# Cross-attention scores from float32r parts of queries and keys, three products in place of one float32 product

## What is computed

```python
q = (layernorm(x) @ Wq.T + bq).reshape(B, L, 16, 16)       # L = 64 queries
k = (ctx @ Wk.T + bk).reshape(B, S, 16, 16)                # S = 256 keys
v = (ctx @ Wv.T + bv).reshape(B, S, 16, 16)
scores = einsum('blhe,bshe->bhls', q, k)
attn = softmax(scores * 16 ** -0.5, axis=-1)
x = x + einsum('bhls,bshe->blhe', attn, v).reshape(B, L, 256) @ Wo.T + bo
```

## Time and profile before

| what | us |
|---|---|
| median of 3 runs | 950.61 |
| lowest and highest of these | 948.52, 951.25 |
| the profiled execution, its time | 948.79 |
| the profiled execution, its span (first to last instruction) | 947.0 |

### The profile page before, as it was taken

One profiled execution on the slowest core, in us unless ns is written; L12 is line 12 of the kernel. 1 busy time (PEld: TensorE's weight loads), 2 busy tenths in 40 slices (PEclk: granted clock), 3 DMA queues, 4 the chain that ended last, 5 costly groups with the idle time before them and its releaser, 6 DMA issues. The chain is left out here.

```text
span 947.0 us, 29217 instructions
## 1 busy us (share of the span) xinstructions
PE 888.6 (94%) x9714; PEld 722.3 (76%) x9730; DVE 790.7 (83%) x1711; ACT 690.9 (73%) x1983; POOL 344.8 (36%) x487
## 2 busy tenths in 40 slices
PE   5899999999999999999999988999999987999997
PEld 4788888888888888888888876878787863555554
DVE  3788878888888888887788877988888876999997
ACT  3587776776777767777677665777777765988887
POOL 1322322223222232224322337767666632222221
PEclk9999999999999999999999999999999997999999
DMA  9111111111111111111111000000000000000001
GB/s 303 37 39 39 43 34 40 40 39 34 39 39 44 39 34 39 39 44 39 34 39 39 28 1 2 1 2 0 1 0 1 2 1 1 28 28 28 28 28 39
DMA packets 31618, 31.64 MB, mean 33 GB/s; under 512 B 3280, under 2 KB 30800, under 8 KB 31568
## 3 DMA queue, kind: packets, MB, share of 16 engines
q1 hardware_dynamic: 30720, 30.73, 10.5%
q10 hardware_dynamic: 848, 0.33, 0.1%
HBM read 26.86 MB, written 4.19 MB: 33 GB/s over the span
## 5 line engine op out<-in xcount | busy, mean ns | idle before, releaser
L485 ACT ACTIVATE probs<-psum,nmax 128x256 f32<-128x256 f32 x512 | 237.8, 488 | 89.6 <-DVE nmax L445 89.6
L445 DVE TENSOR_REDUCE nmax<-psum 128x2 f32<-128x512 f32 x256 | 159.0, 684 | 30.8 <-PE psum L315 30.8
L328 PE MATMUL psum<-id_sb,probs 128*128 128x128 f32 x1024 | 136.4, 277 | 14.3 <-ACT probs L485 14.1
L328 PEld LDWEIGHTS psum<-id_sb,probs 128*128 128x128 f32 x1024 | 111.8, 141 | 30.3 <-ACT probs L485 29.2
L493 POOL TENSOR_TENSOR rstd<-vare,minus_half 128x1 f32<-128x1 f32 x96 | 52.9, 551 | 182.2 <-DVE vare L382 179.7
L502 POOL TENSOR_TENSOR cl<-c_sb,ch 128x512 fp32r<-128x512 f32 x64 | 81.7, 1276 | 99.8 <-ACT ch L460 99.8
L485 ACT ACTIVATION_READ_ACCUMULATOR probs<-psum,nmax 128x1 f32 x512 | 112.7, 220 | 0.0
L466 ACT ACTIVATE probsT<-psum 128x512 f32<-128x512 f32 x160 | 91.0, 625 | 9.0 <-PE psum L328 8.9
L509 POOL TENSOR_TENSOR rm<-rinv,hm_sb 128x256 f32<-128x256 f32 x64 | 39.8, 622 | 127.7 <-DVE rinv L421 127.7
L315 PE MATMUL psum<-k_sb,qb 32*128 32x256 f32 x1024 | 78.4, 404 | 0.0
L1006 PE MATMUL psum<-wb_all,xqT 128*128 128x512 bf16 x240 | 66.2, 390 | 10.3 <-DVE probs L906 7.0
(11 more groups left out here) (126 smaller groups left out, 2303.5 us busy)
## 6 DMA issues: line engine op xcount, KB each, us to landing
c_sb<-in_ctx_t SPq DMA_DIRECT2D x64, 256.0 KB, 2.7
x_sb<-in_x SPq DMA_DIRECT2D x32, 128.0 KB, 2.0
out<-y_sb SPq DMA_DIRECT2D x32, 128.0 KB, 1.7
w_all<-in_w_gate SPq DMA_DIRECT2D x1, 1024.0 KB, 7.9
w_all<-in_w_up SPq DMA_DIRECT2D x1, 1024.0 KB, 10.0
w_all<-in_w_down SPq DMA_DIRECT2D x1, 1024.0 KB, 12.5
wqkv_sb<-in_w_qkv SPq DMA_DIRECT2D x1, 768.0 KB, 6.3
wq_sb<-in_wq ACTq DMA_DIRECT2D x1, 256.0 KB, 3.9
```

The costliest lines, as they stand in the source:

```text
L328: last = nc.tensor.transpose(sp[g][:, c:c + P], probs[:, 2 * g + u, kh * P:(kh + 1) * P], id_sb[:])
L445: nc.vector.tensor_reduce(nmax[:, 2 * g:2 * g + 2], sp[g].rearrange("p (u s) -> p u s", u=2), AX.X, ALU.max, negate=True).then_inc(max_don ...
L485: nc.scalar.activation(probs[:, j, :], sp[g][:, u * S:(u + 1) * S], ACT.Exp, bias=nmax[:, j:j + 1], accum_out=rsum[:, j:j + 1]).then_inc(e ...
```

## The change

Queries and keys are split into a high part in float32r and a low part that holds the rest, and the scores become three float32r products (high by high, high by low, low by high) that accumulate in PSUM. ACT writes the high part of the keys from PSUM with the bias (two instructions of 128x256 a sequence) and the high part of the queries (one of 128x512 a tile). DVE writes the low part of the keys from PSUM (two instructions of 128x256 a sequence in place of one of 128x512). POOL writes the low part of the queries (one of 128x512 a tile). The scores wait for the low parts. In the order of the engines, the new ACT steps stand ahead of the copies to probsT; on DVE, the keys of sequence 1 move from ahead of the reciprocals and the first copy to probsT to behind them. To make room in SBUF, kbd4 now lies in the first part of w_all, and POOL waits for the quantized weights before it writes there.

```diff
@@ names
-        qb = [sb(f"qb{m}", [P, 2, 2, L]) for m in range(KT)]
-        k_sb = sb("k_sb", [P, KT, S])
+        qb = sb("qb", [P, KT, 2, 2, L])
+        qh, ql = sb("qh", [P, KT, 2, 2, L], F32R), sb("ql", [P, KT, 2, 2, L], F32R)
+        kh_sb, kl_sb = sb("kh_sb", [P, KT, S], F32R), sb("kl_sb", [P, KT, S], F32R)
-        kbd4 = [sb(f"kbd4{s}", [P, KT, 4, P]) for s in range(2)]
+        kbd4 = [w_all[:, 2 * i:2 * i + 2, :].rearrange("p k (h t) -> p k h t", h=4) for i in range(2)]
@@ pe_scores
-            pe.wait_ge(qb_done, t * 4 + 4)
+            pe.wait_ge(ql_done, t + 1)
             pe.wait_ge(k_ev, b + 1)
             for m in range(KT):
+                for n, (q, k) in enumerate(((qh, kh_sb), (qh, kl_sb), (ql, kh_sb))):
+                    for c in range(4):
+                        if m + n == 0 and (not isinstance(b, int) or b > 0):
+                            moved, count = pt_count(t + s - 1, 1 - s, c)
+                            pe.wait_ge(moved, count)
+                        rows = slice(32 * c, 32 * c + 32)
+                        last = nc.tensor.matmul(sp[c][:, m * S:(m + 1) * S],
+                                                q[rows, m, s, :, :].rearrange("p h q -> p (h q)"),
+                                                k[rows, m, :], start=n == 0, stop=n == 2)
@@ new steps
+        def dve_kl(v, t, s):
+            v.wait_ge(kh_done, (t * 2 + s) * KT + KT)
+            for m in range(KT):
+                last = nc.vector.scalar_tensor_tensor(kl_sb[:, m, :], k_ps[:, m, :], bk_sb[:, m:m + 1],
+                                                      kh_sb[:, m, :].bitcast(F32), ALU.add,
+                                                      ALU.subtract)
+            last.then_inc(k_ev, 1)
+        flat = "p m s h q -> p (m s h q)"
+        def act_qh(a, t):
+            a.wait_ge(qb_done, t * 4 + 4)
+            a.wait_ge(s_mm, t * 8)
+            nc.scalar.activation(qh[:].rearrange(flat), qb[:].rearrange(flat),
+                                 ACT.Copy).then_inc(qh_done, 1)
+        def act_kh(a, t, s):
+            a.wait_ge(k_mm, t * 2 + s + 1)
+            a.wait_ge(s_mm, (t * 2 + s) * 4)
+            for m in range(KT):
+                nc.scalar.activation(kh_sb[:, m, :], k_ps[:, m, :], ACT.Identity,
+                                     bias=bk_sb[:, m:m + 1]).then_inc(kh_done, 1)
+        def pool_ql(p, t):
+            p.wait_ge(qh_done, t + 1)
+            nc.gpsimd.tensor_tensor(ql[:].rearrange(flat), qb[:].rearrange(flat),
+                                    qh[:].rearrange(flat).bitcast(F32),
+                                    ALU.subtract).then_inc(ql_done, 1)
@@ vector body(t)
-                    dve_k(v, t, 1)
                     dve_inverse(v, t, 0)
                     dve_pt(v, t, 0, (0,))
+                    dve_kl(v, t, 1)
                     dve_xn(v, LN1, t + 1, x_sb[:], xt_mm)
@@ vector body(t), later
-                    dve_k(v, t + 1, 0)
+                    dve_kl(v, t + 1, 0)
                     dve_v(v, t + 1, 0)
@@ scalar body(t)
+                    act_kh(a, t, 1)
                     act_pt(a, t, 0)
...
                     act_exp(a, t, 1, (t, 0))
+                    act_qh(a, t + 1)
+                    act_kh(a, t + 1, 0)
                     act_pt(a, t, 1)
@@ gpsimd body(t)
                     pool_c(p, t + 1, 0)
+                    pool_ql(p, t + 1)
                     pool_rm(p, t, 1)
@@ gpsimd, start of the second stage
+                p.wait_ge(wq_step, 36)
                 pool_kbd4(p, 0, 0, 0, 0)
```

More of the change, by code:

```diff
@@ L212, in block_kernel @@
         cl_done = sem("cl_done")
+        qh_done = sem("qh_done")
+        ql_done = sem("ql_done")
+        kh_done = sem("kh_done")
         k_mm = sem("k_mm")
@@ L306, in pe_scores @@
             b = t * 2 + s
-            pe.wait_ge(qb_done, t * 4 + 4)
+            pe.wait_ge(ql_done, t + 1)
             pe.wait_ge(k_ev, b + 1)
             for m in range(KT):
[L310 to L319, removed]
+                for n, (q, k) in enumerate(((qh, kh_sb), (qh, kl_sb), (ql, kh_sb))):
[7 more added lines that the diff above has]
+                                                k[rows, m, :], start=n == 0, stop=n == 2)
+                        if m == KT - 1 and n == 2:
+                            last.then_inc(s_mm, 1)
         def pe_transpose(pe, t, s, groups=range(4)):
@@ L393, in dve_v @@
                                     ALU.add).then_inc(v_ev, 1)
[L395 to L398, removed]
+        def dve_kl(v, t, s):
[5 more added lines that the diff above has]
+            last.then_inc(k_ev, 1)
         def dve_q(v, t):
             v.wait_ge(q_mm, t + 1)
-            v.wait_ge(s_mm, t * 8)
+            v.wait_ge(ql_done, t)
             for m in range(KT):
@@ L405, in dve_q @@
                     nc.vector.tensor_scalar(
[L406 removed]
+                        qb[:, m, :, h, :], q_ps[:, m, :].rearrange("p (s q) -> p s q", s=2),
                         bq_sb[:, m:m + 1], qm_sb[:, h:h + 1], ALU.add,
@@ L1187, in _ @@
                 dve_q(v, 0)
-                dve_k(v, 0, 0)
+                dve_kl(v, 0, 0)
                 v.wait_ge(w1_in, 16 * len(SET1))
@@ L1307, in _ @@
                 act_c(a, 0, 1)
+                act_qh(a, 0)
+                act_kh(a, 0, 0)
                 act_exp(a, 0, 0)
                 def body(t, pieces=None, w2=None):
+                    act_kh(a, t, 1)
                     act_pt(a, t, 0)
@@ L1388, in _ @@
                 pool_c(p, 0, 1)
+                pool_ql(p, 0)
                 def body(t, w2=None):
```

1 line of the change is left out of this document (added).

## The result

| | before | after |
|---|---|---|
| median, us | 950.66 (948.52 to 951.25) | 970.96 (967.83 to 971.59) |
| ratio | | 1.0215, 95% interval 1.0190 to 1.0239 |
| profiled execution: time, span | 948.79, 947.0 | 971.59, 969.7 |

The change makes the kernel 20.3 us slower. The prediction had the direction, but not the size: 958.0, at most 968.5. In experiments 3 and 7 one execution each took 4.7 and 4.6 ms and is left out of their medians and ranges.

A forecast was written before the change was run, and what follows sets the result against it. PE looked like the bound; the prediction turned on 0.52 of slack in ACT's probsT copies before the scores. +0.28 a tile over 31 passages (8.7) plus 0.5 on 948.79 gave 958.0 us (959.8 from the median), range 950.5 to 968.5.

The forecast's parts named there:

- The rounds: Cross-attention scores on PE: six float32r rounds 0.117 apart replace four float32 rounds of 0.22, -0.16 for each call.
- M0 to M1: From sequence 0's first max reduction to sequence 1's, same tile: 9.06 forecast to become 8.90 through shorter scores.
- the much slower rival: Float32r score rounds take 0.22 like float32, by type or non-overlapping loads: 985.9 us, chance 0.08.
- the rule of the Trainium skill: PE weight loads overlap running matmuls only on different row groups; all six rounds' loads would then be paid in full.
- ACT's added 1.22: High queries and two high keys ahead of ACT's three probsT copies: 0.51 + 0.71, ending the copies 7.44 after M1.
- M1 to M0: From sequence 1's first max reduction to sequence 0's in the next tile: 7.96 forecast to become 8.40, +0.44.
- The faster: Rival: probsT copies do not gate the scores, so PE keeps 0.16 in both halves: 938.9 us, chance 0.08.
- the no-change rival: ACT's three added instructions take their shortest spacing, 1.00, so a tile gains 0.06: 951.2 us, chance 0.13.
- Other gates of the same scores, costed at nothing: Low keys on DVE and low queries on POOL, before sequence 0's scores: both hidden by the wait until 7.50.
- The low queries: POOL's subtraction, 5.25 to 6.6 after M1, ending earlier than the keys: no cost.
- the low keys: DVE, done 6.87 after M1, scores may start at 6.93; costs 0.13 only without the copies' wait until 7.50.
- filling and draining: Start and end of the cross-attention stage, where the same steps stand once without a neighbouring tile: 0.5 us added.

The follow-up runs named there:

- experiment 3: Kernel before, with DVE's weight cast moved between value add and max reductions of sequence 0, beside POOL's context subtraction: 953.58 us, ratio 1.0029.
- experiment 7: Kernel of experiment 6 with the two products of sequence 0's output moved behind the low keys, except in tile 8: 945.26 us, ratio 0.9928.
- experiment 5: Kernel before, with DVE writing queries and keys as float32r and three products of the same high parts summed: 944.25 us, ratio 0.9930.
- Experiments 1: Changed kernel with DVE's weight cast moved from ahead of the low keys to behind the max reductions of sequence 0: 961.32 us, ratio 1.0110.
- experiments 2: Changed kernel with POOL making the low queries for half the heads only (128x256), the rest reusing the high part: 960.7 us, one run.
- experiment 6: Changed kernel with high queries copied by DVE, weight clip ahead of the queries, cast behind sequence 0's max reductions: 974.3 us, ratio 1.0254.
- experiment 10: Changed kernel with the late cast, plus the fourth row tile's six rounds behind the other three's, sequence 0 only: 956.52 us, ratio 1.0040.
- experiment 12: Kernel of experiment 10 with PE's waits for the first three banks' copies ahead of those for low queries and low keys: 949.22 us, ratio 0.9988.
- 11: Changed kernel with the late cast, plus the fourth row tile three rounds behind the others, sequence 0 only: 956.85 us, ratio 1.0046.
- 13: Changed kernel with the late cast and its own round order, three bank waits ahead of the low queries' and low keys': 960.38 us, ratio 1.0110.
- experiments 8 and 9: Unaltered repeats for the second pair of profiles, one run each: the changed kernel 971.37 us, the kernel before 952.16 us.

## Why the prediction was right and wrong

**Held.** The rounds: 0.12 apart, so M0 to M1 is 8.90 in after, and PE alone gains 0.16 in either half (experiment 5). With that the much slower rival falls, and so does the rule of the Trainium skill ("TensorE: Matmul & The Clock Gate", Part 3, The mechanism) as weighed there: six rounds on the same four row groups do not pay for their loads in full. ACT's added 1.22: copies end at 7.45 for 7.44. M1 to M0 in ordinary tiles: 8.43 for 8.40, partly by luck, as told below. The faster and the no-change rival fall with it.

**Failed: "Other gates of the same scores, costed at nothing".** The low queries were placed (5.25 to 6.6 after M1) and called hidden, because only their end was asked for. What DVE does meanwhile was not. In 12 tiles it is the weight cast, in the same window, 0.11 after POOL's start. The cast is shut out until POOL is done, and pushes the low keys from about 318.98 (the high keys end at 318.95) to 319.80. That is 0.75 a tile more than elsewhere, 12 x 0.75 = 9.0 us of the 11.2 by which 970.96 lies above the forecast made from the median (959.8). Experiments 1 to 3 show it from three sides. The Trainium skill has the rule ("SBUF — State Buffer", SBUF: two separate sides): VectorE and GpSimd share a pair of ports, and a VectorE operation in a two-port mode, or with two SBUF inputs against a GpSimd operation that reads SBUF, is locked out until the other's whole instruction ends. The trace agrees: cast 1.47, with half the POOL instruction 0.91, oT 1.13 (experiment 6). That the cast is of the first kind is inferred from its behaviour. In the prediction this would have been a rival of its own: a cast of 0.52 that ends with POOL's 1.28, at 12 tiles.

**Failed in the same part, unseen in the time: the low keys.** They were forecast to let the scores start at 6.93 and to cost 0.13 if the copies' cover were gone. PE starts 0.24 after they end and not 0.06, at 7.15, and its loads then stand 0.16 and 0.11 apart behind fulfilled waits, before the fourth, which also waits for the third copy. In tile 8, outside the loop, the hand-over is 0.07, near the 0.06 forecast. Without the third copy's gate they cost about 0.47: 8.28 in experiment 10, against 7.81 with PE's part alone; of this the chain is 0.25, as 8.03 in experiment 12 shows. So 8.40 came out right with half of the reason, which is luck: two gates at one instant, of which I had priced one. The error shows in experiments 10 and 11, which relieve ACT's third copy alone.

**Mis-sized: filling and draining.** Given 0.5; the start took 0.9 more in the first pair of profiles and 1.6 in the second, the last passage 0.7. How much of the start is the change's stays open: from 20 to 40 us the granted clock was 0.91 in both profiles of before and 0.83 in both of after, and where it was 1.00 there, M0 of tile 1 comes at 35.88 in experiment 3 (scores as before) and 36.19 in 13 (the changed kernel's). In the last passage DVE's xn stands beside another POOL subtraction of 128x256 (timeline of after, DVE and POOL):

```profile
576.98 0.87 DVE L393 TENSOR_SCALAR xn<-x_all,mv,rstd 128x256 f32<-128x256 f32 x1
...
576.97 0.73 POOL L857 TENSOR_TENSOR cl<-xnT,ch 128x256 fp32r<-128x256 f32 x1 [0.47 <-ACT ch L806]
```

In the first stage of before xn takes 0.40 to 0.41; here it ends 0.15 behind POOL's instruction, and so it does, at 0.49, in the ordinary tiles of after, where M0 to M1 is as forecast all the same. It fits the same cause and part of the 0.7, but this one was not tried by itself.

**Not the change's.** The later stages' 3.3, as experiments 8 and 9 show. The profiled execution of before lies 1.9 under its median, that of after 0.6 above.

Up to the last M1 the ledger gives 12 x 1.21 + 18 x 0.45 - 30 x 0.16 + 0.9 + 0.7 = 19.4 in the first pair of profiles; in the second the last M1 stands at 578.67 and 558.13, 20.5 apart. The medians differ by 20.3.

## What to carry to other kernels

When an instruction is put on POOL, asking whether its end is early enough isn't enough: ask what DVE runs in the same window, and price each instruction there that works from SBUF to SBUF, unless a trace shows it unharmed, at POOL's whole remaining time, with all that is queued behind it. Where a step is costed at nothing because something else covers it, work out its own end with its hand-over too: here two gates ended together, so relieving the third copy alone brought 0.11 to 0.15 a tile of the 0.39 that both brought. Inside a loop, waits that are fulfilled early belong ahead of the wait that comes last (0.25 a tile in experiment 12).

## What the runs showed of the hardware

- A POOL tensor_tensor on SBUF shuts out some DVE instructions until it ends: a 128x512 cast to bf16 (0.42 alone, 1.47), a 128x128 add of two SBUF inputs (0.29, 1.13), a tensor_scalar of 128x3 (0.17, 0.82). The cast ends 0.28 after POOL's in all 12 tiles of before, of after and of experiments 2 and 3, the add 0.15 after it, the small one 0.03. A copy or scalar_tensor_tensor that reads PSUM and a 128x8 reciprocal keep their lengths beside it (experiment 7).
- Behind a wait at which PE stood still, four loads inside the loop, each with a wait that is already fulfilled, stand 0.11 apart (four in 0.52 at 320.89). Where PE was not standing still (558.59), and in tile 8 outside the loop (176.40), the four take 0.22.
- Row-tiled float32r rounds of 256 columns stand 0.12 apart on the same four row groups, with one matmul 0.28 long.
- The same stages took 388.61 and 392.27 us in two executions of one kernel, with the granted clock at 0.98 and 0.97 of 2.4 GHz.
